# A macaron block on one core: VectorE's order in the feed-forward groups, the plane differences and attention's rounds

## The reference

```
x = x + 0.5 * ffn(layernorm(x))
x = x + attention(layernorm(x))
x = x + 0.5 * ffn(layernorm(x))

ffn(x):  routing = softmax(x @ gate_w.T)            # 8 experts
         out = (x * (routing @ in_scale)) @ sign(weight).T * (routing @ out_scale) + bias
attention(x): x = conv1d(x, 3 taps, 1024 -> 768) + b; q, k, v = split(x)   # 256 each
         q, k, v projected to 16 heads of 64; causal softmax attention in blocks of 128 tokens
         out = (o @ wo + bo) @ proj_w + proj_b
```

## Time and profile before

| what | value |
| --- | --- |
| median of 3 runs | 1007.85 us (1007.11 to 1010.7) |
| the profiled execution | 1010.62 us, its span 1008.8 us |
| granted TensorE clock, mean | 0.978 |
| busy share: PE, PEld, DVE, ACT, POOL | 91%, 69%, 70%, 41%, 38% |
| phase one's groups | about 0 to 240 us |
| convolution | about 240 to 473 us |
| attention | about 473 to 829 us |
| phase two's groups | about 850 to 1009 us |

### The profile page before, as it was taken

One profiled execution on the slowest core, in us unless ns is written; L12 is line 12 of the kernel. 1 busy time (PEld: TensorE's weight loads), 2 busy tenths in 40 slices (PEclk: granted clock), 3 DMA queues, 4 the chain that ended last, 5 costly groups with the idle time before them and its releaser, 6 DMA issues.

```text
span 1008.8 us, 15266 instructions
## 1 busy us (share of the span) xinstructions
PE 913.5 (91%) x4992; PEld 697.5 (69%) x4992; DVE 705.3 (70%) x1473; ACT 418.6 (41%) x1127; POOL 386.3 (38%) x323
## 2 busy tenths in 40 slices
PE   3788889898989999999989998999999788999997
PEld 2466767675433678788777786878777566887885
DVE  5778777669998897656486488189369847667552
ACT  3533333221134435334675356256535544434331
POOL 2154444546643331000136136134333442554565
PEclk8799999999999999999999999999999899999999
DMA  9432332333223342584203033213152484333432
GB/s 293 157 126 107 105 114 91 108 125 106 73 98 130 137 157 74 191 288 156 74 1 105 1 84 91 58 42 90 48 144 64 171 259 134 126 126 147 140 111 105
DMA packets 43011, 119.97 MB, mean 119 GB/s; under 512 B 7232, under 2 KB 16448, under 8 KB 41536
## 3 DMA queue, kind: packets, MB, share of 16 engines
q1 hardware_dynamic: 42944, 119.11, 35.8%
HBM read 87.64 MB, written 31.46 MB: 118 GB/s over the span
## 4 chain that ended last, share of the span: by engine, by line
PE 53%; DVE 18%; issue 15%; POOL 8%; ACT 3%; DMA 3%; SPq 0%; POOLq 0%; DVEq 0%; ACTq 0%
PE a_p_g L634 11%; PE a_p_g L1848 10%; PE f_p_m L634 6%; PE c_p_m L1292 4%; PE c_p_m L1294 3%; PE c_p_m L1295 3%; PE c_p_m L1296 3%; POOL a_s L1582 3%; POOL a_residual L1569 2%; PE a_p_s L1872 2%; DVE f_nst L399 1%; PE a_p_o L1896 1%; DVE c_ring_f L964 1%; PE a_p_s L577 1%; POOL c_xs_lo L1564 1%
## 5 line engine op out<-in xcount | busy, mean ns | idle before, releaser
L1582 POOL TENSOR_TENSOR a_s<-a_s,a_sums 128x512 f32<-128x512 f32 x64 | 66.6, 1040 | 251.6 <-DVE a_sums L1757 251.6
L280 POOL TENSOR_TENSOR f_y<-f_y,f_res 128x512 f32<-128x512 f32 x64 | 84.4, 1319 | 144.1 <-DVE f_y L492 143.5
L1652 ACT ACTIVATE a_s<-a_s,a_nmx 128x128 f32<-128x128 f32 x256 | 99.3, 390 | 41.8 <-DVE a_nmx L1753 41.8
L634 PE MATMUL f_p_m<-f_wsign,f_a_hi 128*128 128x512 f32 x256 | 106.0, 414 | 0.0
L634 PE MATMUL a_p_g<-f_wsign,f_a_hi 128*128 128x512 f32 x256 | 102.6, 401 | 0.0
L634 PE MATMUL f_p_m<-f_wsign,f_a_lo 128*128 128x512 f32 x256 | 102.1, 399 | 0.0
L634 PE MATMUL a_p_g<-f_wsign,f_a_lo 128*128 128x512 f32 x256 | 100.5, 393 | 0.0
L1848 PE MATMUL a_p_g<-c_xs_hi,x_room 128*128 128x512 f32 x256 | 94.3, 416 | 2.1 <-POOL c_xs_lo L1564 1.8
L277 POOL TENSOR_TENSOR f_res<-f_res,f_hbias 128x512 f32<-128x512 f32 x64 | 84.0, 1313 | 8.4 <-DMA f_res<-x_after_attention 6.3
L1292 PE MATMUL c_p_m<-c_vf,c_ring_f 128*128 128x512 f32 (+1 forms) x192 | 74.2, 543 | 7.2 <-DVE c_ring_f L964 7.2
L1294 PE MATMUL c_p_m<-c_vh,c_ring 128*128 128x512 f32 x192 | 75.5, 393 | 5.2 <-issue 2.9
(11 more groups left out here) (222 smaller groups left out, 2184.7 us busy)
## 6 DMA issues: line engine op xcount, KB each, us to landing
c_raw<-in_conv_w_dram SPq DMA_DIRECT2D x24, 768.0 KB, 4.3
f_w_raw<-in_w_t_dram SPq DMA_DIRECT2D x8, 1024.0 KB, 10.1
f_res<-in_x_dram SPq DMA_DIRECT2D x16, 512.0 KB, 4.3
x_after_ffn<-f_y SPq DMA_DIRECT2D x8, 1024.0 KB, 6.3
f_xin<-x_after_attention SPq DMA_DIRECT2D x8, 1024.0 KB, 5.1
f_res<-x_after_attention SPq DMA_DIRECT2D x16, 512.0 KB, 4.2
out_dram<-f_y SPq DMA_DIRECT2D x8, 1024.0 KB, 6.3
f_xin<-in_x_dram SPq DMA_DIRECT2D x7, 1024.0 KB, 5.1
```

The source lines that it names most:

```text
L280: pool.tensor_tensor(y[:, p, t, h], y[:, p, t, h], res[:, t, h], ALU.add).then_inc(y_done, 1)
L634: last = pe.matmul(p_m[:, q % 2, :], part[p][:, k, q // 2 * P:q // 2 * P + P], wsign[:, k, q % 2 * HALF:q % 2 * HALF + HALF], start=(k == ...
L1582: pool.tensor_tensor(s[:, r], s[:, r], sums[:, r].unsqueeze(2).broadcast_to([P, 4, P]), ALU.mult).then_inc(probs_ready, 1)
L1652: done = act.activation(s[:, r, h, :], s[:, r, h, :], ACT.Exp, bias=nmx[:, r, h:h + 1], scale=SCALE, accum_out=sums[:, r, h:h + 1])
```

## The change

Phase one and two, VectorE's `body`: the pieces of a quarter stand in another order, and long ones are cut into a half for each token tile (`out_stats`, `out_normalise`, `normalise`, `softmax` begin and end). Phase one: planes 2 and 3 are copied as they are by ScalarE for groups 0 to 5, and GpSimd takes the differences of a whole group two groups later; groups 6 and 7 keep VectorE's differences. SP fetches the first half of res first. ScalarE's order in quarters 1 and 3 changes. Attention: four of group 0's v products move from ahead of it into its rounds; the last group's projections, the splits and phase two's start move to other rounds. Cut to its core:

```diff
 # GpSimd
+        def differences(g):
+            quads = bass.ds(g * (FTOK // 4) + 1, FTOK // 4)
+            pool.wait_ge(n_copied, 4 * g + 5)
+            for to, of in ((2, 0), (3, 1)):
+                last = pool.tensor_tensor(Xp[:, :, to, quads], Xp[:, :, to, quads], Xp[:, :, of, quads], ALU.subtract)
+            last.then_inc(differenced, 1)
 # GpSimd body: after q 0's res + bias: differences(g - 2), then nrstd's power (it stood ahead of q 0)
 # SP body
+            if exists(g - 1):
+                sp.wait_ge(y_done, 4 * g - 2)
+                load_res(g, 0)
...                                     # filters (last group), load_x(g + 4)
             if exists(g - 1):
+                sp.wait_ge(y_done, 4 * g)
+                load_res(g, 1)
                 store(g - 1, 1 - p)
 # VectorE body, for q in range(4):
+                first, second = 2 * q, 2 * q + 1
+                after = X is not None and exists(g - 1)
                 if exists(g + 1):
+                    scale(g + 1, 1 - p, first)
+                if q == 0 and after:
+                    out_stats(g - 1, 1 - p, 0)
+                if q == 1 and exists(g + 2):
+                    softmax_begin(g + 2)
+                if q >= 2 and exists(g + 1):
+                    low(g + 1, 1 - p, first - 1)
+                if q == 2 and after:
+                    out_normalise(g - 1, 1 - p, 0)
+                if q == 3 and exists(g + 4):
+                    tile_stats(g + 4, p, 0)
+                if exists(g + 1):
+                    low(g + 1, 1 - p, first)
+                if q == 0 and after:
+                    out_stats(g - 1, 1 - p, 1)
+                    out_mean_var(g - 1)
+                if q == 1 and exists(g + 2):
+                    softmax_end(g + 2)
+                if q == 2 and after:
+                    out_normalise(g - 1, 1 - p, 1)
+                if exists(g + 1):
+                    scale(g + 1, 1 - p, second)
+                if q == 0 and exists(g + 3):
+                    normalise_tile(g + 3, 1 - p, 0)
+                if q == 3 and exists(g + 4):
+                    tile_stats(g + 4, p, 1)
+                if q in (0, 3) and exists(g + 1):
+                    low(g + 1, 1 - p, second)
+                if q == 0 and exists(g + 3):
+                    normalise_tile(g + 3, 1 - p, 1)
+                if q == 3 and exists(g + 4):
+                    mean_var(g + 4)
+                if q == 1 and X is not None and late(g):
+                    dve.wait_ge(differenced, NG - 2)
                     conv.early_data(dve, Xp, 0)
+                if q == 3 and X is not None and late(g):
+                    difference(g - 1, 0)
+                    last_stats(0)
+                    difference(g - 1, 1)
+                    conv.first_filter(dve, 0, 0)
+                    difference(g - 1, 2)
+                    conv.first_filter(dve, 0, 1)
+                    difference(g - 1, 3)
 # last_normalise(0) now follows the loop; then early_data 1 as before
 # ScalarE
+            planes = slice(0, 2) if by_two(g) else slice(0, 4)          # by_two: g >= NG - 2
+            act.copy(plane_part(g, c, planes), normed_planes(g, c)[:, :, planes, :]).then_inc(n_copied, 1)
 # body: q 1: exponent(g + 2) ahead of high(2q + 1); q 3: copy_normed(2) ahead of it too
 # TensorE, normed(g, p, c)
+            if by_two(g) and (g, c) != (NG - 2, 0):
                 pe.wait_ge(t_copied, 4 * NG)
+                wait(pe, n_differenced, 4 * (g - NG + 2) + c - 1)
+            else:
+                wait(pe, n_copied, 4 * g + c + 1)
 # attention
-        for n, u in enumerate((1, 3, 5, 7, 9, 11, 12, 13)):
+        for n, u in enumerate((1, 3, 5, 7, 12, 13, 14, 15) if last else (1, 3, 5, 7, 9, 11, 12, 13)):
             rounds[u].append(("proj", -1, n))
+    if first:
+        for n in range(GT):
+            rounds[n].append(("v", 0, GT + n))
-            rounds[14 + n].append(("qk", 1, part))
+            rounds[(13 if first else 14) + n].append(("qk", 1, part))
-BEFORE = [("qk", 0, part) for part in range(4)] + [("v", 0, n) for n in range(2 * GT)]
+BEFORE = [("qk", 0, part) for part in range(4)] + [("v", 0, n) for n in range(GT)]
-SPLIT_ROUNDS = (11, 11, 13, 13, 15, 16)
+SPLIT_ROUNDS = (10, 11, 12, 13, 14, 15)
 # ScalarE: split_high of a round stands behind that round's oT copy (L1676), not ahead of it
 # ScalarE, last group: copy_t(1, 1, 2) and (1, 1, 3) behind all of `after`, not ahead of taking wo 1
 # GpSimd, last group: power(1) behind the rounds, not in round 8
 # VectorE, last group: tile_stats(0, 0, t) in rounds 0 and 1 (before 0 and 2); and behind the rounds:
+                if last:
+                    for t in range(FT):
+                        s2.tile_stats(1, 1, t)
+                    s2.mean_var(1)
+                    s2.round_scales()
+                    for t in range(FT):
+                        s2.normalise_tile(1, 1, t)
+                    s2.part_scales()
```

More of the change, by code:

```diff
@@ L392, in low, with out_stats, out_mean_var @@
                               ALU.subtract).then_inc(lo_done, 1)
[L394 to L400, removed]
+        def out_stats(g, p, t):
+            dve.wait_ge(y_done, 4 * g + 2 * t + 2)
+            if t == 0:
+                wait(dve, y_normed, g + 1)
+            for h in range(2):
+                last = dve.bn_stats(nst6[:, t, h, :], y[:, p, t, h * HALF:h * HALF + HALF])
+            if t == FT - 1:
+                last.then_inc(n_stats, 1)
+        def out_mean_var(g):
             dve.wait_ge(n_stats, g + 1)
@@ L457, in body @@
                     difference(g - 1, 1)
[L458 to L468, removed]
@@ L469, in body @@
-                if q == 3 and exists(g + 1):
-                    low(g + 1, 1 - p, KD - 1)
-                if q == 3:
-                    for t in range(FT):
-                        if exists(g + 4):
-                            tile_stats(g + 4, p, t)
-                        if X is not None and exists(g - 1):
-                            difference(g - 1, 2 + t)
-                        if X is not None and late(g):
-                            (last_stats, last_normalise)[t](0)
-                    if exists(g + 4):
-                        mean_var(g + 4)
@@ L1591, in body @@
                         s2.power(0)
-                    if last and u == 8:
-                        s2.power(1)
                 if last:
@@ L1658, in body @@
                             take(g, n + 1, flat(first, last).index(step) % 2, step)
-                    for c in range(NCH):
-                        if not last and u == SPLIT_ROUNDS[c]:
-                            reader = ("qk", 0, 4 * QUADS - 2 + c // 2) if c < 2 * WC else ("proj", -1, 2 * GT - 1)
-                            if reader in flat(first, last):
-                                act.wait_ge(gen_full, number(g, first, last, reader) + 1)
-                            split_high(g + 1, c)
                     if last and u >= UNITS:
@@ L1677, in body @@
                                            bias=bvs[:, 2 * quad + i:2 * quad + i + 1]).then_inc(o_hi, 1)
+                    for c in range(NCH):
+                        if not last and u == SPLIT_ROUNDS[c]:
+                            reader = ("qk", 0, 4 * QUADS - 2 + c // 2) if c < 2 * WC else ("proj", -1, 2 * GT - 1)
+                            if reader in flat(first, last):
+                                act.wait_ge(gen_full, number(g, first, last, reader) + 1)
+                            split_high(g + 1, c)
                 for step in after:
```

88 lines of the change are left out of this document (38 added, 50 removed).

## The result

The changed kernel takes 1001.4 us (median of 20 runs, 998.63 to 1003.09), the kernel before 1007.88 in 20 runs beside it: ratio 0.9936, interval 0.9922 to 0.9949. The forecast was 982 us with 972 to 999 as its range; the time lies outside it. In the profiled executions it is 1001.46 against 1010.62 us.

What follows compares the result with a forecast made beforehand. TensorE, busy 913.5 of 1008.8 us, was taken to bound the kernel, leaving at most 95 us. Terms summed to -27.7, cut by 1.7 for overlapping stops to -26 us: 982 us forecast, range 972 to 999.

Steps and rivals of the forecast that it cites:

- Phase one's groups: Six feed-forward groups: VectorE's new order and differences moved to GpSimd win 16.5 us, bounds -21 and 0.
- the transposes' wait: Phase one: transposes of normalised rows waited 7.8 us for VectorE's differences; about 6 go, 0.3 us a group kept.
- Differences on GpSimd: Phase one: VectorE loses 1.7 us a group; GpSimd gains two operations of 1.29 us each, costing VectorE little.
- Rival 1: Phase one: GpSimd's 12 new operations slow both neighbours, VectorE late again; feed-forward gives 8, 995 us; chance 0.23.
- Rival 2: Attention: loads come too late, ScalarE sits for split chunks twice in each of three groups; 1004 us; chance 0.07.
- End of phase one: Phase one's end into the convolution: earlier statistics free VectorE's last product sooner; -1 us (+2 to -3).
- Group 0: Attention's first group: v products fill a wait, next group's qk starts in round 13; -3 us (0 to -6).
- Groups 1 and 2: Attention's middle groups: splits moved so their load chain starts a round sooner; -2.4 us (+5 to -6).
- Last rounds: Attention's last group: statistics and normalisations leave VectorE's full rounds, two projection additions move later; -4.5 us (0 to -9).
- Its tail: After the last attention group's rounds: later VectorE work balanced by fewer ScalarE copies; 0 us (+3 to -1).
- The new wait of 1 to 2 us: Last attention group's tail: predicted sign, a new wait ahead of the second tile's transposes.
- Phase two: Feed-forward groups after attention: already at full speed; -0.3 us, bounds 0 and -0.8.

Runs made afterwards that it cites:

- experiment 7: Changed kernel with next group's products from round 14 in group 0, plus ScalarE's first copy ahead of its casts in phase one: 991.01 us, ratio 0.9826.
- experiment 8: Changed kernel with next group's products from round 14 in group 0, plus phase one's plane differences on VectorE instead of GpSimd: 996.36 us, ratio 0.9881.
- experiment 1: Only the feed-forward half of the change; attention and its tail as in the kernel before: 992.79 us, ratio 0.985.
- experiment 2: Changed kernel, but the next group's q and k products begin in round 14 of attention's group 0, not round 13: 993.98 us, ratio 0.9871.
- experiment 6: Changed kernel with next group's products from round 14 in group 0, plus last group's projection additions back in their old rounds: 993.27 us, ratio 0.9851.
- experiment 3: Changed kernel, but GpSimd's four last-group bias additions wait for the second wo result: 999.22 us, ratio 0.9909.
- experiment 4: Changed kernel, but SyncE issues the feed-forward weights' loads ahead of attention's last residual store of group 2: 999.19 us, ratio 0.9927.
- experiment 5: Changed kernel with products from round 14 in group 0, weights' loads ahead of the last store, and GpSimd's four additions behind the second wo result: 988.09 us, ratio 0.9791.

## Why the prediction was wrong, by its own steps

- **Phase one's groups, -16.5, measured -12.3.** VectorE's order did what was laid out: a_lo's 8.8 us fell to 2.3. The mis-sized term is the transposes' wait: "copy and handovers, 0.60 + 0.3, just fit". The copy took 0.615 us as priced, but I counted only what lies between two transposes, not ScalarE's queue ahead of the first of them. 6.0 us stayed where I left 1.8, and those 4.2 are the whole miss of this term; experiment 7 shows half of the 6.0 to be that queue. Full groups took 25.1 us, not 22.9 to 23.6.
- **Differences on GpSimd.** Priced at 1.29 each, measured 1.305. I had VectorE at 19.3 us in a full group; it is 21.3. The new operations cost it 3.8 us in all, on one 2-element operation a group, which I had not priced; the rest came from the reordering, whose new neighbours the layout left out: the halves of y's normalising (1.43 us each for 0.97) and a 16-element operation (1.03 for 0.17) now lie beside GpSimd's old additions (experiment 8). Rival 1 had the mechanism, but not the place, for phase one won more than its 8 us. Rival 2's time, 1004, came nearest to 1001.4, and by luck: ScalarE never sat 2.4 us for a split chunk.
- **End of phase one, -1, measured -3.5**, past its bound of -3. TensorE's wait for the last normalised rows is 0.85 us, 1.54 before. Experiment 1 has -3.3 with the feed-forward half alone; which of its edits gave the rest was not separated.
- **Group 0, -3, measured +4.9.** The failed sentence is: "It needs the lower part of chunk 1, which the earlier splits give only at about that wait's end, so one product's 1.4 us is won." The arrival was right (512.52, TensorE idle from 509.0). What I left out is what stands behind the product in TensorE's queue. The transposes and value products of the round, which did not need chunk 1, waited too, and the loop through VectorE and GpSimd made the next lower part late as well. Experiment 2: 6.3 us. Without it the term would have been -1.4, for the v products alone.
- **Groups 1 and 2, -2.4.** Measured -1.3, but the traces can't tell it from nothing. All ten with the new split rounds have a TensorE wait of 1.9 to 2.3 us in either group; behind it the granted clock sometimes falls (0.60 in group 2 after) and sometimes does not (1.00 in group 1 after), and a group then takes about 86.1 or 84.6 us. So they lie between 169.2 and 172.3 us, and the two with the old rounds at 168.8 (experiment 1) and 171.9. Rival 2's stop is there in small: with the new rounds ScalarE waits 1.0 to 1.2 us for conv_out's loads twice in each of the two groups, with the old ones (experiment 1) once, and the TensorE wait of 2.0 us that I meant to remove is in both groups of the new rounds and not in experiment 1. The term has no support.
- **Last rounds, -4.5, measured -4.4.** Experiment 6 gives at least 3.7 us of it to the statistics; that the projections' place gave anything is not shown.
- **Its tail, 0 (+3 to -1), measured +7.3.** Two sentences failed. "GpSimd's four bias additions start 2.3 us later and are still in time" was blind to whom they hold up: 4.33 us, experiments 3 and 4. The 2.3 was right by itself (2.2 against round 14 in experiment 6, behind the power), but the additions started 6.4 us later, since the loads of their rows stood behind the same store as the weights. And ScalarE's copies were weighed without SyncE's queue: the late projection holds the store, the store the weights (797.26, 2.8 us behind round 14, before; 786.11, 8.3 us behind it, after), the weights ScalarE: 2.83 us, experiments 4 and 6. The new wait of 1 to 2 us that I did forecast, for the second tile, is there with 0.47.
- **Phase two, -0.3, measured +0.3:** none.

So the steps that failed are group 0's early product and the tail's cover, 15.2 us together; phase one's wait is a term of the right kind and 4.2 us too small. With the first two mended, as in experiment 5, the kernel takes 988.1 us, at the edge of the forecast's own range of 975 to 989: the two terms are the whole of the miss beyond it.

The Trainium skill, "SBUF — State Buffer", section "SBUF: two separate sides", says that VectorE and GpSimd share one port pair as a lock for a whole instruction, and that VectorE's fast modes and operations with two SBUF inputs are what it hits. The traces agree: the copy, cast and two-input operation are let go at the additions' ends, while in experiment 3 the statistics (2.47 us) and the projection's additions out of TensorE's result (0.68 us), which then ran beside GpSimd's, kept their lengths. In the same run the 2-element operation on SBUF (1.80 us for 0.17) did not. The prediction named this rule and set it against the long halves of phase one and the new operations alone.

## What to carry to other kernels

When a step moves earlier in an in-order queue, list what stands behind it there, and do not credit the step with filling a wait that it may itself wait through. When a step moves later, follow every queue that waits for it, the one that issues loads included. And when a long GpSimd instruction moves, ask which of VectorE's SBUF operations it will lie beside: the smallest ones can cost most for their size, since each may wait for a whole neighbour. That holds for VectorE's work moved beside GpSimd's as well as the other way round.

## What the runs showed of the hardware

A VectorE operation of 2 to 16 elements a partition took 0.17 us alone and, beside GpSimd additions of 1024 elements (2.3 us each), 1.80 us (2 elements, experiment 3) and 1.93 to 2.27 (16 elements); a normalising pair took 1.53 us alone and 5.52 beside them. The additions suffer too: 4.63 us for two beside small operations, 6.11 beside long ones. Letting them start 3.6 us earlier against round 14 moved the loss to another operation and kept its size (4.33 and 4.50 us of TensorE's waiting). Putting them mostly beside statistics and additions out of TensorE's result, whose lengths did not change, left 0.93 us of it. The same stop of TensorE was followed by the low clock in one execution and not in another: behind a wait of 2.75 us the 16 value products took 1.98 us in experiment 1 and 1.09 in experiment 2. Two repairs of one stretch, worth 4.2 and 0.9 us alone, gave 7.1 together.
